# A layer kernel's routing: eight-largest group sums in all blocks, block results in place, and a new table of places for the routing steps

## The reference

```python
x = x + attn_ref(layernorm(x), Wq, bq, Wk, bk, Wv, bv, Wo, bo, gamma, beta)   # 16 heads of 64, post-norm inside
x = x + ffn_ref(layernorm(x), router_w, e_bias, Wg, Wu, Wd, SWg, SWu, SWd)

def route(x, router_w, e_bias):                     # 64 experts in 8 groups of 8
    scores = sigmoid(x @ router_w.T)
    sfc = scores + e_bias
    group_scores = top_k(sfc.reshape(T, 8, 8), 2)[0].sum(-1)     # the sum of each group's two largest
    gidx = top_k(group_scores, 4)                                # four groups stay
    masked = where(in those groups, sfc, 0)
    idx = top_k(masked, 8)                                       # eight experts of a token
    w = scores[idx]; return idx, 2.5 * w / (w.sum + 1e-20)

coef[token, idx] = w
h = silu(x @ Wg[e]) * (x @ Wu[e]) * coef[:, e];  moe = sum_e h @ Wd[e]
out = moe + silu(x @ SWg) * (x @ SWu) @ SWd         # a shared expert beside them
```

## Time and profile before

| what | value |
|---|---|
| three runs | 1283.54, 1283.19, 1282.24 us; median 1283.19 |
| the profiled execution | 1283.23 us, of which 1281.4 us are the span from first to last instruction |
| PE busy | 1229.8 us, 96% of the span |
| DVE busy | 1086.8 us, 85% |
| POOL busy | 986.5 us, 77% |
| ACT busy | 884.5 us, 69% |
| DMA packets of SP's queue | 49.6% of the time of the 16 DMA engines |
| idle time of PE that DVE's L1114 ended | 10.5 us in 17 waits |
| granted PE clock | 0.997 of full speed on average |

### The profile page before, as it was taken

How to read it: one execution, slowest core, us unless ns; L and a number is a source line. 1 busy time by engine, 2 the same in 40 slices (tenths; PEclk the granted TensorE clock), 3 DMA queues, 4 the chain that set the end, 5 groups by cost and what they waited for, 6 DMA issues and landing times. The chain is left out here.

```text
span 1281.4 us, 33475 instructions
## 1 busy us (share of the span) xinstructions
PE 1229.8 (96%) x12473; PEld 684.4 (53%) x12473; DVE 1086.8 (85%) x1997; ACT 884.5 (69%) x1586; POOL 986.5 (77%) x1183
## 2 busy tenths in 40 slices
PE   4999999999999999999999799999999999999998
PEld 1466666666666666666665554444444444444443
DVE  6788888888888998898999788888888888888875
ACT  4688877777777778777776566666666666657564
POOL 2788888888888988898888386768676776768675
PEclk9999999999999999999999899999999999999999
DMA  7455565555555565565564253534343434344352
GB/s 184 98 107 113 106 113 107 113 110 109 113 106 120 108 112 107 113 106 113 106 107 88 68 150 97 169 112 152 125 144 124 151 121 138 129 125 140 115 158 86
DMA packets 186862, 152.59 MB, mean 119 GB/s; under 512 B 104721, under 2 KB 143953, under 8 KB 186705
## 3 DMA queue, kind: packets, MB, share of 16 engines
q1 hardware_dynamic: 186704, 150.50, 49.6%
HBM read 80.16 MB, written 3.15 MB: 65 GB/s over the span
## 5 line engine op out<-in xcount | busy, mean ns | idle before, releaser
L1147 PE MATMUL bank<-arena 128*128 128x65 f16 (+3 forms) x12344 | 1219.5, 264 | 39.2 <-DVE arena L1114 10.5
L1147 PEld LDWEIGHTS bank<-arena 128*128 128x128 f16 (+2 forms) x12344 | 669.2, 98 | 576.7 <-issue 90.0
L541 POOL TENSOR_TENSOR arena<-arena 128x512 f16<-128x512 f32 x504 | 537.5, 1091 | 89.7 <-ACT arena L692 89.3
L577 POOL TENSOR_TENSOR arena<-arena 128x256 f16<-128x256 f32 x528 | 343.5, 675 | 149.8 <-ACT arena L753 143.3
L692 ACT ACTIVATE arena<-bank 128x512 f32<-128x512 f32 x512 | 291.6, 595 | 125.5 <-PE bank L1147 112.8
L1020 DVE TENSOR_REDUCE arena<-bank 128x2 f32<-128x1024 f32 x256 | 311.7, 1219 | 44.6 <-PE bank L1147 44.5
L753 ACT ACTIVATE arena<-arena 128x512 f16<-128x512 f32 x264 | 164.6, 624 | 138.3 <-DVE arena L1114 137.4
L1106 DVE TENSOR_TENSOR arena<-arena,bank 128x512 f32<-128x512 f32 x256 | 174.5, 682 | 48.1 <-PE bank L1147 28.1
L1114 DVE TENSOR_TENSOR arena<-arena,bank 128x512 f32<-128x512 f32 x264 | 181.8, 689 | 38.6 <-ACT bank L748 15.3
L748 ACT ACTIVATE bank<-bank 128x512 f32<-128x512 f32 x264 | 153.2, 580 | 64.1 <-PE bank L1147 63.6
L1029 DVE SCALAR_TENSOR_TENSOR arena<-bank,arena 128x512 f16<-128x512 f32 x128 | 95.5, 746 | 20.3 <-ACT arena L682 20.0
(11 more groups left out here) (103 smaller groups left out, 379.5 us busy)
## 6 DMA issues: line engine op xcount, KB each, us to landing
arena<-coef_rows SPq DMA_DIRECT2D x512, 128.0 KB, 3.0
arena<-arena SPq DMA_DIRECT2D x256, 128.0 KB, 2.4
arena<-arena SPq DMA_DIRECT2D x64, 256.0 KB, 3.1
arena<-in_L_attn_x SPq DMA_DIRECT2D x9, 256.0 KB, 3.9
arena<-in_L_ffn_Wg SPq DMA_DIRECT2D x32, 64.0 KB, 2.3
arena<-in_L_ffn_Wu SPq DMA_DIRECT2D x32, 64.0 KB, 2.2
arena<-in_L_ffn_Wd SPq DMA_DIRECT2D x32, 64.0 KB, 2.2
arena<-arena SPq DMA_TRANSPOSE x128, 3.4
```

The lines of the kernel that those rows point to most:

```text
L541: last = pool.tensor_tensor(num_lo[:, u % 2, s, h, :], num[:, u % 2, s, h, :], num_hi[:, u % 2, s, h, :, 1], ALU.subtract)
L577: last = pool.tensor_tensor(hid_lo[:, r, at], hid[:, r, at], hid_hi[:, r, at], ALU.subtract)
L1147: return nc.tensor.matmul(out_, lhsT, rhs, start=start, stop=stop, skip_group_check=True)
```

## The change

The change has five parts. (1) The group sums of blocks 1 to 7 are done as those of block 0, by `max` in eight parts of four; steps 17 and 18 are gone. (2) `x2` of block n lies in the block's own rows of `xn` (block 0 keeps a buffer of its own), so that POOL's wait for `out_sent` is gone. (3) The tables: steps 7 to 14 move two to four tiles forward, 16 is spread over tiles 15 to 21, PE's transposes of the coefficients stand behind tile 25, ACT's copy of them behind tile 30; block 0 gets a set of tables of its own (`DVE_1` and so on) for the routing of block 1. (4) At the turn of the stages: ACT's steps 11, 14 and 30 of block 0 stand one slot earlier, DVE's tail pieces one tile earlier, the first ahead of tile 1 and of steps 1 and 2, and SP writes block 0's coefficients and spreads those of tiles 1 and 2 ahead of `turn` of pair 63. (5) SP loads a block's input two blocks ahead, at tile 20.

```diff
-ACT_0 = {(41, 3): (4,), (42, 3): (5,), (51, 3): (9,), (52, 3): (10,), (53, 1): (11,), (54, 1): (14,), (63, 1): (30,)}
+ACT_0 = {(41, 3): (4,), (42, 3): (5,), (51, 3): (9,), (52, 3): (10,), (53, 0): (11,), (54, 0): (14,), (63, 0): (30,)}
 PE_0 = {(53, 0): (8,), (54, 0): (11,), (63, 0): (27,)}
...
-DVE_N = {0: (1, 2), 1: (3,), 9: (7,), 10: (8,), 15: (12,), 19: (16,), 20: (17,), 21: (18, 19), 22: (20,),
-         23: (21,), 24: (23, 24), 25: (25,), 26: (26,), 27: (27, 28)}
-POOL_N = {3: (3,), 4: (2,), 6: (5,), 7: (6,), 10: (8,), 17: (14,)}
-ACT_N = {5: (4,), 6: (5,), 12: (9,), 13: (10,), 15: (11,), 18: (14,), 32: (30,)}
-PE_N = {11: (8,), 13: (11,), 27: (27,)}
+DVE_N = {0: ((1, None), (2, None)), 1: ((3, None),), 6: ((7, 0),), 7: ((7, 1),), 8: ((8, None),), 11: ((12, 0),),
+         12: ((12, 1),), 15: ((16, 0),), 16: ((16, 1),), 17: ((16, 2),), 18: ((16, 3),), 19: ((16, 4), (16, 5)),
+         20: ((16, 6),), 21: ((16, 7), (19, None)), 22: ((20, None), (21, 0)), 23: ((21, 1), (23, None)), 24: ((24, None),),
+         25: ((25, None),), 26: ((26, None),), 27: ((27, None), (28, None))}
+POOL_N = {1: (3, 2), 4: (5,), 5: (6,), 8: (8,), 13: (14,)}
+ACT_N = {3: (4,), 4: (5,), 9: (9,), 10: (10,), 11: (11,), 14: (14,), 30: (30,)}
+PE_N = {7: (8,), 9: (11,), 25: (27,)}
...
+POOL_1 = {3: (3,), 4: (2,), 5: (5,), 6: (6,), 8: (8,), 15: (14,)}
+ACT_1 = {4: (4,), 5: (5,), 10: (9,), 11: (10,), 13: (11,), 16: (14,), 30: (30,)}
+PE_1 = {9: (8,), 11: (11,), 26: (27,)}
...
-ACT_TAIL = {4: ((65, 2),)}
-DVE_TAIL = {1: ((64, 1), (64, 2)), 2: ((64, 3),), 4: ((65, 0), (65, 2)), 8: ((66, 0),), 11: ((67, 0),)}
+ACT_TAIL = {3: ((65, 2),)}
+DVE_TAIL = {0: ((64, 1),), 1: ((64, 2),), 2: ((64, 3),), 3: ((65, 0),), 4: ((65, 2),), 7: ((66, 0),), 10: ((67, 0),)}
...
+        def x2(m):
+            return x2_0 if isinstance(m, int) and m == 0 else xn[:, m * QT:(m + 1) * QT, :]
...
+                if p == PAIRS - 1:
+                    sp.wait_ge(coef_sb, 1)
+                    sp.dma_start(coef_hbm[0], coef_rows[0]).then_inc(coef_out, 16)
+                    sp.wait_ge(scores_t, 8 * (PAIRS - 2))
+                    sp.wait_ge(coef_out, 16)
+                    for k in (1, 2):
+                        spread(0, k)
                 turn(p, u)
...
-                    wait(pool, out_sent, (m - 1) * 16)
                     pool.wait_ge(xbeta, m + 1)
                     pool.wait_ge(gained, m + 1)
-                    pool.tensor_tensor(x2[r], ya, xin[r], ALU.add).then_inc(x2_done, 1)
+                    pool.tensor_tensor(x2(m), ya, xin[r], ALU.add).then_inc(x2_done, 1)
...
-                if k == 16 and m == 0:
+                if k == 16:
                     dve.wait_ge(sfc_done, m + 1)
                     for g in range(4 * part, 4 * part + 4):
                         own(nc.vector.max(ranked[:, g, :], g8[:, g, :]))
-                if k == 19 and m == 0:
+                if k == 19:
                     own(nc.vector.tensor_reduce(gsum, ranked[:, :, 0:2], AX.X, ALU.add))
-                if k == 16 and m > 0:
-                    dve.wait_ge(sfc_done, m + 1)
-                    own(nc.vector.tensor_tensor(hi4, g8[:, :, 0:4], g8[:, :, 4:8], ALU.max))
-                    own(nc.vector.tensor_tensor(lo4, g8[:, :, 0:4], g8[:, :, 4:8], ALU.min))
...
             def run_block(n, r, last):
+                if n == 0:
+                    tail(run, DVE_TAIL[0])
                 if not last:
                     for part in DVE_N[0]:
-                        route(n + 1, 1 - r, part)
+                        route(n + 1, 1 - r, *part)
```

More of the change, by code:

```diff
@@ L162, in layer @@
         ya = tiles4(take(S))
-        x2 = [tiles4(take(S))]
+        x2_0 = tiles4(take(S))
         assert top[0] <= xT_hi_at + dead
@@ L446, in send @@
                 sp.wait_ge(out_ready, n + 1)
-                sp.dma_start(ov[rows(n)].rearrange("o p t d -> p (o t) d"), x2[r]).then_inc(out_sent, 16)
+                sp.dma_start(ov[rows(n)].rearrange("o p t d -> p (o t) d"), x2(n)).then_inc(out_sent, 16)
             def run_block(n, r, last):
[L450 to L456, removed]
+                if n > 0:
+                    sp.wait_ge(coef_sb, n + 1)
+                    sp.dma_start(coef_hbm[r], coef_rows[r]).then_inc(coef_out, 16)
+                    sp.wait_ge(coef_out, n * 16 + 16)
+                for k in range(1 if n > 0 else 3, TILES):
                     if k > 4:
                         sp.wait_ge(prod_done, n * TILES + (k - 3))
-                    elif later:
+                    elif n > 0:
                         sp.wait_ge(prod_done, n * TILES + (k - 4))
[L462 to L466, removed]
+                    spread(r, k)
+                    if k == 4 and n == 0:
                         load_x(1, 1)
                         turn(PAIRS, PAIRS % HP)
-                    if k == 8 and not later:
+                    if k == 7 and n == 0:
                         turn(PAIRS + 1, (PAIRS + 1) % HP)
-                    if k == 2 and not last and later:
-                        load_x(n + 1, 1 - r)
-                    if k == 8 and later:
+                    if k == 8 and n > 0:
                         send(n - 1, 1 - r)
+                    if k == 20 and n + 2 < B:
+                        load_x(n + 2, r)
             blocks(sp, run_block)
@@ L582, in run_block @@
                     if not last:
-                        for part in POOL_N.get(k, ()):
+                        for part in (POOL_N if n else POOL_1).get(k, ()):
                             route(n + 1, 1 - r, part)
@@ L651, in route @@
                     for t in ((0, 1) if k == 9 else (2, 3)):
-                        last = nc.scalar.activation(xf[:, t, :], x2[r][:, t, :], ACT.Identity,
+                        last = nc.scalar.activation(xf[:, t, :], x2(m)[:, t, :], ACT.Identity,
                                                     bias=shift[:, t:t + 1], scale=rstd[:, t:t + 1])
@@ L768, in run_block @@
                     if not last:
-                        for part in ACT_N.get(k, ()):
+                        for part in (ACT_N if n else ACT_1).get(k, ()):
                             route(n + 1, 1 - r, part)
@@ L1415, in run_block @@
                     if not last:
-                        for part in PE_N.get(k, ()):
+                        for part in (PE_N if n else PE_1).get(k, ()):
                             route(n + 1, 1 - r, part)
```

32 lines of the change are left out of this document (11 added, 21 removed), and 3 rows, old and new, of the table DVE_1.

## The result

The changed kernel took 1271.78 us (median of four, 1271.65 to 1272.14) against 1282.72 us of the kernel before (four, 1280.76 to 1283.54): a ratio of 0.9917, interval 0.9900 to 0.9935. That is 10.9 us less, where 4.2 were forecast. The profiled execution took 1272.14 us, its span is 1270.3 us (before: 1281.4), so 11.1 us are to be found.

| stretch of PE's list | before | after | gain | forecast |
|---|---|---|---|---|
| to a score matmul near attention's end | 700.16 | 697.92 | 2.2 | 2.6 |
| from there to the end of tile 9's down in block 0 | 758.10 (761.99 less two tiles) | 752.60 | 3.3 | 3.5 |
| from there to the transposes of block 0's sum (L1405, now L1409) | 808.5 | 800.9 | 2.1 | 1.2 |
| from there to the end | 1281.4 | 1270.3 | 3.5 | 0.9 |
| falls of the clock in new waits | | | (in row 2) | -4.0 |

The account below looks back on a forecast made before the run. PE, busy 96% of the span, bounds the kernel, so only its idle or slow time can go. Attention -2.6, turn -3.5, block 0 -1.2, later blocks -0.9: -8.2; clock +4: -4.2 from 1283.2, forecast 1279.0 us, range 1270 to 1287.

Parts of the forecast that it names:

- the first rival: PE's clock never falls in the new waits: 1283.2 - 8.2 = 1275; chance 0.2.
- the second division: Turn of the stages: PE waits some 2.4 us for DVE's second division of context, leaving 3.5 us off there.
- step 8: PE's transposes of the normalised input, now behind tile 7: PE idles 1.7 to 1.8 us in each of blocks 1 to 6.
- 1.03: DVE's first scalar instruction of step 8: taken as 0.17 us; 1.03 if POOL is still busy, making the wait 2.6.
- the slower rival: Step 8's chain longer (5.4 us) and clock falls in most new waits (10): 1290, or 1286 with half; chance 0.2.
- The walk: Block 2's chain to PE's step 8 on the old trace's clock: POOL ends tile 7 at 887.2, DVE's instruction starts 887.3.
- One in three: Clock falls behind one in three of seven new waits: 2.3 falls, 4 us; bounds none and all seven (12 us).
- "+0.3": PE's transposes of the coefficients behind tile 25: 0.3 us of wait in blocks 1 to 6, near 0.8 in block 0.
- a block's old losses: Second stage: a block loses about 2.2 us, two waits for `hid` with their 0.16 being 1.7, the rest small delays.
- "Group sums": Eight-largest over seven tiles replace thirteen instructions in three; waits at block ends and starts go, 2.2 us off per block.
- "1.4 + 2.8 - 1.7": DVE's lateness at tile 22 before the change: 2.5 us, of which 1.4 from ACT's sigmoid delaying silu; now 0.4.
- in place at nothing: In-place results change nothing the trace shows anyone waiting for; POOL's step 6 never stood waiting for `out_sent`.

Follow-up runs that it names:

- experiment 10: Changed kernel with the early steps (3, 2, 5 to 14) of blocks 2 to 7 back where the kernel before has them, eight-largest form kept: 1274.94 us, 0.9947.
- 1: Kernel before with attention's edit alone (ACT's steps 11 and 14 of block 0 one slot earlier): 1279.37 us, 0.9973.
- experiment 11: Changed kernel with POOL's step 6 again waiting until the result of two blocks before has been sent: 1276.26 us, 0.9952.
- experiment 4: Changed kernel with PE's step 8 one tile earlier in blocks 1 to 6 (behind tile 6, not 7): 1292.19 us, 1.0074.
- 7: Changed kernel with PE's steps 8 and 11 one tile later and group sums by the thirteen comparisons: 1264.21 us, 0.9865.
- 5: Changed kernel with the group sums of blocks 1 to 7 done again by the thirteen comparisons, at tiles 19 to 21: 1273.82 us, 0.9936.
- Experiment 3: Changed kernel with PE's step 8 behind tile 8, not 7, and its step 11 behind tile 10, not 9, in blocks 1 to 6: 1264.92 us, 0.9876.
- experiment 8: Changed kernel with PE's steps 8, 11 and 27 each one tile later, eight-largest group sums kept: 1260.16 us, 0.9839.
- 12: Changed kernel with PE's steps 8, 11 and 27 each one tile later and group sums by the thirteen comparisons: 1260.07 us, 0.9827.
- 2: Kernel before with the turn's edits alone (SP's order, ACT's step 30, DVE's tail pieces): 1278.53 us, 0.9971.

## Why the prediction was right or wrong

**Right: the way, and the waits one by one.** The time lies in the range, faster as forecast. It is 7.2 us below the forecast of 1279.0, though, and the first rival (1275, no fall in the new waits) came nearer: the wrong terms below nearly all erred to the same side, and it is the width of the range that held them. Attention gave 2.4 by the waits (2.6 taken). PE waits 2.5 us for the second division (2.4 forecast) and 1.59 us by the rows at step 8 of each of blocks 1 to 6 (1.6 forecast). The largest new cost was thus foreseen to a tenth, by following one chain across three engines on the old trace's clock. DVE's waits for coefficients (19.5 us in 10 in the kernel before) are gone, as forecast.

**Right, by little: L942 at step 8.** It took 0.17 us in each of the six blocks, so the 1.03 that the slower rival needed did not come back. POOL's last tile had ended at 879.80, 0.04 us ahead of it (0.04 to 0.05 in all six). The walk gave 0.1, less than it could tell, so this was in part luck. With the early steps back in their old places (experiment 10) the same line took 1.13 to 1.14 us in all six. At the turn the same line did meet POOL (timelines of DVE and POOL):

```profile
728.31 0.51 DVE L942 TENSOR_SCALAR arena<-arena 128x4 f32<-128x4 f32 x1
728.85 0.59 DVE L944 TENSOR_SCALAR arena<-arena 128x4 f32<-128x4 f32 x1
...
728.12 1.29 POOL L598 TENSOR_TENSOR arena<-arena 128x256 f16<-128x256 f32 x2 [1.85 <-ACT arena L774]
```

Each of the two ends with one of POOL's two instructions (728.79 and 729.42, to 0.03 us) and takes three times its 0.17 or more. The Trainium skill ("SBUF — State Buffer", "Who interferes with whom") says that a `tensor_scalar` of DVE can need the ports that it shares with POOL, and that the one that issues first then holds them for its whole instruction while the other waits; these rows agree.

**Mis-sized: the clock, 4.0 us.** "One in three" of seven waits should have cost 2.3 falls; one fell, at the turn, and two that the kernel before had there were gone, of which I had counted one. The level is not decided by the wait alone. Over the fourteen traces: the 1.64 us ahead of 710 were followed by the lower level in 3 of 14 (before, 1, 11), the 2.52 for the second division in 4 of 10 (the change, 4, 7, 10), the first division's 4.7 to 4.9 in 2 of 2. In the second stage waits were followed by it in none of 18 cases of 1.6 us (six each in the change, 5 and 10), in none of six of 1.7 to 2.5 (11) and in five of six of 3.53 (4). My single row of a fall came from the turn, and I carried a third of its odds to a stage where waits of this size brought none.

**Wrong: "+0.3" at step 27 in blocks 1 to 6, 1.8 us.** It was added to the 1.75 at step 8, but PE meets both in one block: held back by the first it comes later to the second. Experiment 3 shows the pair: without the first, the second is 0.6 to 1.0. The same sum took 2.2 us for a block's old losses. By the starts they were 2.4: the six blocks from 808.51 to 1217.50 (L1405) are 68.17 each, and a block of experiment 8, in which PE has no wait listed, is 65.76. Block 0 the same: 2.5 lost before instead of 2.0, and 0.43 at step 27 instead of 0.8.

**Wrong: the cause of the old waits.** "Group sums" credited the eight-largest in pieces with a block's 2.2 us. The waits did go, but not for that: 5, 7 and 12 put the comparisons back and the waits stay away, 10 puts the early steps back and the loss returns with the eight-largest in place. In "1.4 + 2.8 - 1.7" the 1.4 (ACT's sigmoid) was the part that moved: four tiles earlier, DVE has recovered from it when the sums begin (rows of 7). Open ends remain: in 10 the loss stands at step 27, which is two tiles earlier than before, and no longer at `hid`, so that it is the same loss is argued from its size (67.95 beside 68.00) and from ACT's rows. That early steps alone would do, with the later steps where they were, was not run.

**Wrong: in place at nothing.** POOL's step 6 never waited for the DMA in the kernel before, but its new place is two tiles earlier, where it would: 2.2 us by the rows of 11. The earlier loads of x were not run by themselves; no list of waits, before or after, names a wait for them in the second stage.

**The slower rival** did not come because L942's 1.03 did not come back. What it would have cost is not shown: its wait of some 2.6 us lies between those of 1.7 to 2.5, after which the clock stayed up (experiment 11), and those of 3.53, after which it fell in five of six. With these, one tile more, waits and falls together cost 3.4 us a block (experiment 4, 20.4 over six), and the kernel is slower than before (1.0074).

## What to carry to other kernels

Before a step is moved, follow its whole chain across the engines with durations of the old trace: that gives a new wait to a tenth of a us, and says by how many tiles the consumer must move with the producer. Do not add waits of one engine within one period: take the later one as what remains after the earlier, and expect that removing the first uncovers the second (10.5 us became 6.3 here by the waits, and moving the second step by a tile gave 4.7 more). When a change alters an instruction and its place together, undo each by itself before saying which of them paid.

## What the runs showed of the hardware that was not expected

The lower clock level came in some traces and not in others behind the same wait at the same place (1.64 us: 3 of 14; 2.52 us: 4 of 10), and nearly always behind 3.53 us (5 of 6); one fall cost 1.55 to 1.69 us. A single trace with or without a fall is no evidence on an edit: kernels that differ nowhere near it differ by that much (7 fell at 732, 8 did not). Between 18 and 42 us, where PE often waits, the clock was 0.50 in five of the fourteen traces (1, 2, 4, 7, 11) and 1.00 in the others. Those five have mean clocks of 0.982 to 0.990, the others 0.997 and more; the change's four executions have 0.998, 0.998, 0.988 and 0.988 and took the same within 0.5 us, so a low clock there costs nothing that can be seen.
